# Attention of a graph network: the counts' logarithms added by GpSimd instead of the tensor engine

## What is computed

```python
e = leaky_relu(al_s[src] + al_d[dst], 0.2)
m = segment_max(e, dst)
ex = exp(e - m[dst])
z = segment_sum(ex, dst)
out = segment_sum(h[src] * (ex / z[dst])[:, :, None], dst)
```

## Time and profile before

| what | us |
|---|---|
| median of three runs | 2178.45 |
| the profiled execution | 2181.19 |
| its span | 2179.4 |
| tensor engine busy | 1939.9 (89%) |
| VectorE busy | 1211.6 (56%) |
| ScalarE busy | 838.8 (38%) |
| GpSimd busy | 559.0 (26%) |

### The profile page before, as it was taken

How to read it: one execution, slowest core, us unless ns; L and a number is a source line. 1 busy time by engine, 2 the same in 40 slices (tenths; PEclk the granted TensorE clock), 3 DMA queues, 4 the chain that set the end, 5 groups by cost and what they waited for, 6 DMA issues and landing times.

```text
span 2179.4 us, 34673 instructions
## 1 busy us (share of the span) xinstructions
PE 1939.9 (89%) x11166; PEld 1699.0 (78%) x11167; DVE 1211.6 (56%) x2275; ACT 838.8 (38%) x1125; POOL 559.0 (26%) x538
## 2 busy tenths in 40 slices
PE   5998998989999999779999999996788869878898
PEld 5887986759999977579999999996446857675676
DVE  7842223454443645565555655554555687756696
ACT  2221222332222223224555555553333128631676
POOL 0003765630000056434333444100772000000000
PEclk9999999999999999989999999998899989989999
DMA  5445667754556567657788887875883012100211
GB/s 163 151 154 167 178 170 259 267 163 127 168 168 196 172 232 246 197 175 236 263 274 267 276 265 253 285 236 184 266 271 126 8 37 61 66 15 8 68 61 54
DMA packets 203766, 377.74 MB, mean 173 GB/s; under 512 B 18937, under 2 KB 174378, under 8 KB 203670
## 3 DMA queue, kind: packets, MB, share of 16 engines
q1 hardware_dynamic: 171014, 245.57, 34.9%
q0 software_dynamic: 31216, 128.89, 18.7%
q10 hardware_dynamic: 1440, 1.97, 0.2%
HBM read 288.03 MB, written 88.33 MB: 173 GB/s over the span
## 4 chain that ended last, share of the span: by engine, by line
PE 38%; DVE 6%; issue 5%; DMA 4%; ACT 3%; another core or an unknown queue 1%; POOL 1%; ACTq 0%; SPq 0%; DVEq 0%; POOLq 0%
PE ps L1867 20%; PE ps L2084 4%; PE ps L2049 3%; DMA arena<-in_L_gnn_W_rel 3%; PE ps L1749 2%; PE ps L1896 2%; PE ps L2126 1%; PE ps L1744 1%; PE ps L2010 1%; PE ps L1669 1%; DMA arena<-U,ix 1%; DVE arena L1471 1%; POOL arena L529 1%; PE ps L2036 1%
## 5 line engine op out<-in xcount | busy, mean ns | idle before, releaser
L1867 PE MATMUL ps<-w_hi,hT_hi 128*128 128x384 f32 x2052 | 719.5, 351 | 45.8 <-ACT arena L615 13.8
L1867 PE MATMUL ps<-w_hi,hT_lo 128*128 128x384 f32 x2052 | 695.0, 339 | 0.3 <-issue 0.3
L1867 PE MATMUL ps<-w_lo,hT_hi 128*128 128x384 f32 x2052 | 694.9, 339 | 0.0
L1867 PEld LDWEIGHTS ps<-w_hi,hT_hi 128*128 128x128 f32 x2052 | 391.8, 191 | 55.8 <-issue 19.3
L1867 PEld LDWEIGHTS ps<-w_lo,hT_hi 128*128 128x128 f32 x2052 | 391.5, 191 | 0.4 <-issue 0.2
L529 POOL DMA_INDIRECT arena<-U,ix x252 | 272.1, 1080 | 465.4 <-DMA U<-arena 348.6
L1867 PEld LDWEIGHTS ps<-w_hi,hT_lo 128*128 128x128 f32 x2052 | 391.3, 191 | 0.0
L615 ACT ACTIVATE arena<-ps 128x384 f32<-128x384 f32 x160 | 78.2, 492 | 448.4 <-PE ps L1867 386.4
L1749 PE MATMUL ps<-arena,onehot 128*128 128x512 f32 x504 | 197.6, 516 | 20.1 <-DVE onehot_r L1087 7.5
L1749 PEld LDWEIGHTS ps<-arena,onehot 128*128 128x128 f32 x504 | 91.0, 199 | 99.9 <-issue 95.8
L565 POOL DMA_INDIRECT h<-h_d,lidx x68 | 91.5, 1346 | 295.6 <-PE ps L1896 252.0
(11 more groups left out here) (289 smaller groups left out, 2920.6 us busy)
## 6 DMA issues: line engine op xcount, KB each, us to landing
arena<-in_L_gnn_W_rel SPq DMA_DIRECT2D x74, 1152.0 KB, 6.2
U<-arena SPq DMA_DIRECT2D x292, 192.0 KB
arena<-in_L_gnn_W SPq DMA_DIRECT2D x36, 1152.0 KB
U<-z SPq DMA_DIRECT2D x28, 864.0 KB
arena<-rows_d SPq DMA_DIRECT2D x40, 320.0 KB, 3.4
arena<-in_L_gnn_root SPq DMA_DIRECT2D x4, 1152.0 KB
arena<-U,ix POOLq DMA_INDIRECT x252
arena<-in_L_gnn_W_root SPq DMA_DIRECT2D x2, 1152.0 KB
```

What stands on the lines that cost most here:

```text
L1867: ins = pe.matmul(acc, l, r[:, j, kt, :], start=(n == 0), stop=(n == 3 * KT - 1))
```

## The change

`log_terms` is replaced by `row_terms`: two matmuls per head, ones times `mrow`, into the PSUM buffer of that head (`terms(hd % 2)`), issued at tile 3 of the head before. GpSimd adds the logarithms: for each tile it waits for `z_ok`, adds `CT[:, t]` to `zt[:, t]` in place and adds one to a new semaphore `g_ok`. VectorE waits for `g_ok` instead of `z_ok`, and for `c_ok` only at the first tile of a head. The splits of the logarithms, their buffers, their semaphores and the fp32r identity go. The operations of `maximum`, `z`, `e` and `head_out` are unchanged.

```diff
@@ GpSimd, behind the last gathers @@
+            def log_counts(n, it, m):
+                for i in range(m):
+                    t = i % NG
+                    pool.wait_ge(A[n]["z_ok"], 2 * NG * it + i + 1)
+                    pool.tensor_tensor(zt[:, t, :], zt[:, t, :], CT[:, t, :], ALU.add).then_inc(A[n]["g_ok"], 1)
+            pool.wait_ge(S["ct_ln"], 1)
+            for n in range(3):
+                if n == 1:
+                    log_counts(n, 0, NG)
+                else:
+                    with pool.Fori(0, HEADS[n][0] // 2) as it:
+                        log_counts(n, it, 2 * NG)
@@ ScalarE @@
-            def logs(n, ts=range(NG)):
-
-                for t in ts:
-                    act.activation(cl_hi[:, t, :], CT[:, t, :], cp).then_inc(S["cl_hi"], 1)
...
-            act.wait_ge(S["ct_ln"], 1)
-            logs(0)
             rows(0)
...
-            logs(1, range(3))
             rows(1)
-            logs(1, (3,))
             spread(rowS, 6, A[1]["rs0"], 1)
-            logs(1, (4,))
             spread(rowD, 2, A[1]["rd0"], 2)
@@ VectorE, logits @@
-                dve.wait_ge(s["z_ok"], k + 1)
-                dve.wait_ge(s["c_ok"], k + 1)
+                dve.wait_ge(s["g_ok"], k + 1)
+                if t == 0:
+                    dve.wait_ge(s["c_ok"], 2 * it + i // NG + 1)
                 z = zt[:, t, :].rearrange("p (b n) -> p b n", b=2)
-                dve.tensor_tensor(z, z, terms(i % 2), ALU.add).then_inc(s["l_ok"], 1)
+                dve.tensor_tensor(z, z, terms(i // NG), ALU.add).then_inc(s["l_ok"], 1)
@@ VectorE, logs(0), logs(1, range(4)) and logs(1, (4,)) and their function go @@
-                    dve.wait_ge(S["cl_hi"], NG * n + t + 1)
-                    ins = dve.tensor_tensor(cl_lo[:, t, :], CT[:, t, :], cl_hi[:, t, :].bitcast(F32), ALU.subtract)
@@ tensor engine @@
-            def log_terms(n, it, i):
+            def row_terms(n, hd):
 
                 s = A[n]
-                j, t = i // NG, i % NG
-                if t == 0:
-                    pe.wait_ge(s["row_cp"], 2 * (2 * it + j) + 3)
-                if not (isinstance(it, int) and it == 0 and i < 2):
-                    pe.wait_ge(s["l_ok"], 10 * it + i - 1)
-                for m, (l, r) in enumerate(((ident_r, cl_hi[:, t]), (ident_r, cl_lo[:, t]), (ones_r, mrow[:, j]))):
-                    for b in range(2):
-                        ins = pe.matmul(terms(i % 2)[:, b, :], l[:], r[:, NP // 2 * b:NP // 2 * (b + 1)], start=(m == 0), stop=(m == 2), skip_group_check=True)
+                pe.wait_ge(s["row_cp"], 2 * hd + 3)
+                if hd >= 2:
+                    pe.wait_ge(s["l_ok"], NG * (hd - 1))
+                for b in range(2):
+                    ins = pe.matmul(terms(hd % 2)[:, b, :], ones_r[:], mrow[:, hd % 2, CW * b:CW * (b + 1)], start=True, stop=True)
                 ins.then_inc(s["c_ok"], 1)
...
-                        if k + 2 < NG * H:
-                            log_terms(n, (k + 2) // (2 * NG), (k + 2) % (2 * NG))
+                        if t == 3 and hd + 1 < H:
+                            row_terms(n, hd + 1)
```

More of the change, by code:

```diff
@@ L95, in gnn_kernel @@
         mx_scr = [arena[:, o:o + NP] for o in (7040, 9600, 10240)]
-        with nc.sbuf_tensor("ident_r", [P, P], F32R) as ident_r:
-            with nc.sbuf_tensor("ones_r", [P, P], F32R) as ones_r:
-                pass
+        with nc.sbuf_tensor("ones_r", [P, P], F32R) as ones_r:
+            pass
         with nc.sbuf_tensor("onehot_r", [P, MB, P], F32R) as onehot_r:
@@ L107, in parts_of @@
             return (late_hi, late_lo) if ph == 2 else (msg[:, 0], msg[:, 1])
-        cl_hi, cl_lo = (t[:].rearrange("p j k n -> p (j k n)")[:, 0:NG * NP].rearrange("p (g n) -> p g n", g=NG) for t in (w_hi, w_lo))
         counts = sb("counts", [P, 2, NG, NP])
@@ L250, in gnn_kernel @@
         g_in = [sem(f"g_in{b}") for b in range(RB)]
-        A = [{m: sem(f"{m}_{n}") for m in ("al_ok row_tp row_cp row_st rs0 rd0 mx mx_ok cl_ok c_ok z_ok l_ok p_ok o_mm o_ev"
+        A = [{m: sem(f"{m}_{n}") for m in ("al_ok row_tp row_cp row_st rs0 rd0 mx mx_ok g_ok c_ok z_ok l_ok p_ok o_mm o_ev"
                                            + (" rs1 rd1 o_cp o_tp o_r" if n != 1 else "")).split()} for n in range(3)]
@@ L1446, in scores @@
                 link(ins)
-            def logs(n, ts=range(NG)):
-                for t in ts:
-                    dve.wait_ge(S["cl_hi"], NG * n + t + 1)
-                    ins = dve.tensor_tensor(cl_lo[:, t, :], CT[:, t, :], cl_hi[:, t, :].bitcast(F32), ALU.subtract)
-                if NG - 1 in ts:
-                    ins.then_inc(A[n]["cl_ok"], 1)
             def maximum(n, it, j, groups):
@@ L1593, in _ @@
             link(ins)
-            logs(1, range(4))
             maximum(1, 0, 0, range(NG))
-            logs(1, (4,))
             for t in range(NG):
@@ L2037, in head_rows @@
                 ins.then_inc(s["row_tp"], 1)
-            def log_terms(n, it, i):
+            def row_terms(n, hd):
                 s = A[n]
-                j, t = i // NG, i % NG
-                if t == 0:
-                    pe.wait_ge(s["row_cp"], 2 * (2 * it + j) + 3)
-                if not (isinstance(it, int) and it == 0 and i < 2):
-                    pe.wait_ge(s["l_ok"], 10 * it + i - 1)
-                for m, (l, r) in enumerate(((ident_r, cl_hi[:, t]), (ident_r, cl_lo[:, t]), (ones_r, mrow[:, j]))):
-                    for b in range(2):
-                        ins = pe.matmul(terms(i % 2)[:, b, :], l[:], r[:, NP // 2 * b:NP // 2 * (b + 1)], start=(m == 0), stop=(m == 2), skip_group_check=True)
-                ins.then_inc(s["c_ok"], 1)
-            def first_terms(n):
-                if n < 2:
-                    pe.wait_ge(A[n]["cl_ok"], 1)
-                for i in range(2):
-                    log_terms(n, 0, i)
+                pe.wait_ge(s["row_cp"], 2 * hd + 3)
[3 more added lines that the diff above has]
+                    ins = pe.matmul(terms(hd % 2)[:, b, :], ones_r[:], mrow[:, hd % 2, CW * b:CW * (b + 1)], start=True, stop=True)
+                ins.then_inc(s["c_ok"], 1)
             def tiles_(n):
@@ L2064, in tiles_ @@
                     pe.sem_inc(s[m], v)
-                first_terms(n)
+                row_terms(n, 0)
                 def turned(hd):
@@ L2115, in _ @@
                 head_rows(1, 0, part)
-            first_terms(1)
-            for i in range(2, NG):
-                log_terms(1, 0, i)
+            row_terms(1, 0)
             pe.wait_ge(A[1]["p_ok"], NG + 10)
```

4 lines of the change are left out of this document (1 added, 3 removed).

## The result

The changed kernel takes **2231.51 us** (median; runs of 2225.07, 2225.35, 2237.66 and 2238.23) where the kernel before takes 2177.81 in the same session. The ratio is 1.0247, 95% interval 1.0219 to 1.0274: slower, by 54 us where 25 had been forecast.

A forecast was written before the change was run, and what follows sets the result against it. VectorE and the tensor engine were taken to bound attention 2 alike, the tensor engine attention 0; with turns at the SBUF reads, 22 + 7 - 8 + 3 = +24 us gave 2203 us, own range 2190 to 2216 (0.52), whole range 2166 to 2240.

The forecast's parts named there:

- What bounds the kernel before: Attention 2: VectorE limits a head as much as the tensor engine, 10.94 us; attention 0: 10.93, VectorE alone about 10.0.
- What is removed: Four of six logarithm matmuls per tile, some 1.5 of 2.1 us; splits on ScalarE and VectorE priced at nothing.
- The price of one addition: One GpSimd addition of 128x640 fp32 with two SBUF inputs: 1.45 us, between 1.10 and 1.63.
- Turns: In heads with maxima, GpSimd's reads stand still during a VectorE operation with two SBUF inputs; the other direction wasn't shown.
- the sum of what must take turns: Per head with maxima, two-input VectorE operations plus GpSimd's 7.25 us: 12.75 in attention 2, 11.75 in attention 0, plus 0.4.
- The small operations: Five small VectorE operations per head, 0.17 us each, counted as 0.8 us in the turns.
- The last heads: Last two heads of attentions 0 and 2, without maxima: ScalarE comes next, 16.8 us with seams, -4 each, -8.
- Attention 1: One head: additions +0.5 us, line 2126's matmuls partly at the lower clock +2.5; entered as 3.
- nothing overlaps: Rival in heads with maxima: each maximum may wait a whole GpSimd addition; +105, 2284 us, at half 2231; chance 0.18.
- The faster rival: Shared SBUF reads: VectorE and GpSimd read together without blocking; -12.5 us, 2166; chance 0.20.
- The slow tensor engine: Tensor engine at half clock: starts per head under 12 us, only takes back the faster rival's gain; no chance given.

The follow-up runs named there:

- number 2: The changed kernel without GpSimd's additions, the logarithms left out and the mask zero; 0.9927 of the kernel before.
- number 10: The kernel before with one reduction of the row of maxima per head in place of the five maxima; 0.9936 of the kernel before.
- number 4: The changed kernel with ScalarE's relus four tiles ahead instead of three; 1.027 of the kernel before.
- number 6: The changed kernel with each GpSimd addition split into two halves of 320 columns; 1.0192 of the kernel before.
- number 5: The changed kernel with GpSimd's addition replaced by a one-input copy in place, logarithms left out and mask zero; 0.9968 of the kernel before.
- number 3: The changed kernel with each maximum replaced by a max reduction with one SBUF input, GpSimd's additions kept; 1.0151 of the kernel before.
- number 1: The changed kernel unaltered, run again as the mark for the others; 1.0262 of the kernel before.

## Why the prediction was right about the turns and wrong about what they hide

**What bounds the kernel before.** The tensor engine and VectorE level in attention 2: right on both sides, 10.8 us per head with the tensor engine relieved of the logarithms (number 2) and 10.8 with VectorE's lightened (number 10). In attention 0 VectorE alone needs 9.6, not 10.0; that figure stood in two of the rivals and not in the forecast's sum.

**What is removed.** The splits at nothing: right. From the first maximum to the first PSUM addition of attention 0 it takes 14.5 us, 14.1 before. The attention starts 4 us earlier than in the profile of before; its first maximum does so already, so that comes from the layers ahead and not from the change (their last matmul of line 1867, now 1858, starts at 1774.0 instead of 1778.8).

**The price of one addition.** Taken as 1.45 us, measured 1.50 (five in 7.5 us in attention 1), inside the bounds of 1.10 and 1.63. The estimate from the Trainium skill (GPSIMD Engine Reference, Elementwise — side-by-side cycle accounting), 1.4, was a little low. Over five additions that is 0.25 us per head.

**Turns.** That a two-input operation on one engine shuts out the other for its whole length: right, and in both directions, which the trace of before had not shown. The rule of the Trainium skill that was quoted there (SBUF — State Buffer, Who interferes with whom), that the second to start waits for the first to finish, holds for VectorE behind GpSimd too (1.52 us for the maximum at 1828.73).

**The step that failed** is the sum of what must take turns, and the sentence that carries it: "ScalarE makes each relu three tiles ahead, so GpSimd has a backlog that fills the turns." The sum of 12.75 and 11.75 us supposes that GpSimd works whenever VectorE does something harmless, so that VectorE pays only for what doesn't fit. The runs show 14.1 us per head in attention 2 (140.6/10) and 14.2 in attention 0 (85.5/6). For attention 0: VectorE's own pace is 9.6. I sum over its instructions in the order of time what each takes above the shortest of its kind: 21.3 us on 30 maxima and 7.7 on six operations of line 1476, 29.0 in all, 4.8 per head. 9.6 + 4.8 = 14.4, against 14.2. So of GpSimd's 7.5 us per head only 2.7 are hidden, where the forecast had hidden 7.25 - (12.15 - 10.0) = 5.1. In attention 2 the same sum gives 3.5 per head (28.9 on maxima, 3.9, 1.3 and 1.1 on three other lines), and 10.8 + 3.5 = 14.3, against 14.1.

Why so little is hidden: GpSimd waits for a relu ahead of most additions, and the relu comes through ScalarE when VectorE has just finished a PSUM addition. In the rows above GpSimd's starts lie 0.7 us ahead of a maximum, 0.04 behind one, 0.1 ahead of an operation on 128x5. The addition of 1.5 us doesn't fit under a PSUM addition of 0.74 in any case. That the start follows the loop is shown by the waits. How much is its phase and how much its length is argued: a longer lead changed nothing (number 4), shorter pieces helped a little (number 6), and an operation short enough for the place beside a PSUM addition is nearly free though it shuts out as well (number 5).

**The small operations** were counted at their own length, 0.8 us per head. One of 0.16 us can cost 1.5: number 3 shows it best, where the reductions are harmless and heads still take 12.0 instead of 9.6.

**The last heads**, -8 forecast: -5.4 and -2.6, together -8.0. That ScalarE comes next was right too. In attention 0 they took 15.4, close to GpSimd's pace (10 x 1.53), but GpSimd isn't what holds them. Stretches in these heads, first of the changed kernel, then of number 5, where GpSimd only copies:

```profile
1886.00:1900.00 14.00, 11.75 (x49) 6.42 (x47) 8.51 (x16) 13.16 (x20) 10.82 (x8) 1.00 0.01 2
1876.00:1890.00 14.00, 11.68 (x48) 6.46 (x48) 8.32 (x15) 13.16 (x20) 5.06 (x7) 1.00 0.01 2
```

ScalarE is busy 13.16 of 14 us in both, and from first to last addition these two heads take 14.6 us in both, in number 6 (halves) too, and 14.9 without any addition on GpSimd (number 2). In attention 2 the ten steps take 17.5 with GpSimd's additions and without them.

**Attention 1**, +3 forecast: the additions +0.7, the matmuls at the lower clock +2.5 (35.1 - 32.6) as forecast, and yet from the last addition of attention 0 to the first of attention 2 only +1.8 in all.

**The rivals.** The measured 2231.5 lies on the half-way point of the rival "nothing overlaps" (2231), which had 0.18. That it lies just there is chance: the share that is paid differs between the attentions, and number 1 shows longer heads for the same kernel. Its mechanism, a maximum that stands behind a whole GpSimd addition, is the one in the rows: 4.8 of 7.5 us are paid in attention 0 and 3.5 in attention 2. What was said against it, that two PSUM additions or the head's output would hide one whole, is no more than 2.7 of 7.5 us in attention 0. The faster rival, reads that mix, is refuted by the stretched maxima, and with one input on GpSimd they don't mix either (number 5). The slow tensor engine came true as a clock (0.81 and 0.74 in the stretches above) and cost nothing that shows, since that engine idles for a quarter of the time or more.

## What to carry to other kernels

Before work is moved to GpSimd, list the instructions of VectorE beside it that have two inputs in SBUF, whatever their size, and price each at up to one whole GpSimd instruction; a sum of turns is the lower end and holds only if the moved work can start when it likes. Where it stands in a chain with the blocked engine, it starts at the wrong moment again and again, and one tile more of lead didn't mend that. Fewer inputs on GpSimd's side don't mend it either; a shorter operation does. Give VectorE one-input forms first, then move the work, and only in the stages where the engine that is relieved sets the pace. Even that isn't enough: with one reduction per head, attention 0 gained 11.7 us and attention 2, where two larger two-input operations are left per head, lost 5.7.

## What the runs showed of the hardware

- An operation on 128x5 elements with two SBUF inputs took 1.48 us instead of 0.16, and one on 128x320 1.62 instead of 0.49, beside a two-input addition on GpSimd. VectorE's 128x640 addition with one input in PSUM stayed at 807 to 823 ns, and a reduction with one input at 807 to 820.
- GpSimd's addition of 128x640 fp32 takes 1.54 us alone and one every 1.50 us in a row, its copy 0.72. Half the columns take 0.85, and two halves in a row 1.68 instead of 1.54.
- A GpSimd copy with one SBUF input and a VectorE maximum with two shut each other out as well: 1.03 us instead of 0.72 for the copy, 1.33 instead of 0.82 for the maximum (number 5).
- The two engines fall into a repeating pattern: heads of 13.5 us in one profiled execution and 14.8 in another, of the same kernel.
